# Two transformer layers on one core: work dealt out anew between score slots, rows of maxima sent ahead of the stores, the first layer's norm half a turn earlier, fp4 rounding on GpSimd

## The reference, cut to what matters

```python
xn = layernorm(x)
x = x + attention0(xn) + ffn0(xn)       # ffn0: fp4_linear in and out
xn = layernorm(x)
x = x + attention1(xn) + moe(xn)        # moe: shared expert + top 2 of 8 experts

def fp4_quant_dequant(x):               # blocks of 16 along the last dim
    scale = max(max(abs(xb)) / 6, 1e-12)
    xn = xb / scale                     # rounded to 0, .5, 1, 1.5, 2, 3, 4, 6
    return grid(abs(xn)) * sign(xn) * scale
def fp4_linear(x, w): return fp4_quant_dequant(x) @ fp4_quant_dequant(w).T
ffn0(x) = fp4_linear(silu(fp4_linear(x, w_gate)) * fp4_linear(x, w_up), w_down)
```

## Time and profile before

| | |
|---|---|
| median of 3 runs | 1664.07 us (1662.01 to 1670.28) |
| the profiled execution | 1662.64 us |
| its span, first to last instruction | 1660.9 us |
| busy: PE, DVE, ACT, POOL | 1199.5, 1016.8, 723.0, 375.0 us |
| mean granted TensorE clock | 0.868 of full |
| the chain that ended last | PE 27%, DVE 27%, issue 21%, POOL 9% |

### The profile page before, as it was taken

How to read it: one execution, slowest core, us unless ns; L and a number is a source line. 1 busy time by engine, 2 the same in 40 slices (tenths; PEclk the granted TensorE clock), 3 DMA queues, 4 the chain that set the end, 5 groups by cost and what they waited for, 6 DMA issues and landing times.

```text
span 1660.9 us, 18766 instructions
## 1 busy us (share of the span) xinstructions
PE 1199.5 (72%) x6747; PEld 522.3 (31%) x6807; DVE 1016.8 (61%) x1596; ACT 723.0 (44%) x921; POOL 375.0 (23%) x395
## 2 busy tenths in 40 slices
PE   2657478877786788777867887787778858888851
PEld 1113123212321332223212321232223246677510
DVE  7855677766676767666766676777685425411122
ACT  1045044644464446444644464446454713233450
POOL 5020111101110111011101110111001344455475
PEclk9668668987898889878987798889989979999985
DMA  4934232133313321432133213331410363455332
GB/s 135 349 149 115 89 99 83 30 111 82 85 30 107 95 76 30 112 94 73 29 109 85 84 30 106 80 86 30 113 34 14 96 159 122 131 149 163 110 104 69
DMA packets 143230, 159.65 MB, mean 96 GB/s; under 512 B 14585, under 2 KB 132546, under 8 KB 141090
## 3 DMA queue, kind: packets, MB, share of 16 engines
q1 hardware_dynamic: 129986, 123.87, 26.7%
q0 software_dynamic: 12208, 34.04, 6.9%
q10 hardware_dynamic: 944, 0.54, 0.1%
HBM read 90.11 MB, written 67.76 MB: 95 GB/s over the span
## 4 chain that ended last, share of the span: by engine, by line
PE 27%; DVE 27%; issue 21%; POOL 9%; ACT 6%; DVEq 6%; DMA 3%; SPq 1%; ACTq 0%; POOLq 0%
DVE nm L959 13%; PE sums L347 5%; ACT ex L695 3%; PE mx L359 3%; PE ring L458 3%; PE mx L329 3%; PE mx L409 2%; PE mx L449 2%; PE ring L433 2%; POOL qs L1361 2%; POOL ks L1361 2%; PE ring L253 2%; POOL xn L1313 2%; DVEq L914 1%; DVEq L873 1%
## 5 line engine op out<-in xcount | busy, mean ns | idle before, releaser
L695 ACT ACTIVATE ex<-mx 128x1024 f32<-128x1024 f32 x512 | 512.4, 1025 | 505.4 <-PE mx L359 503.0
L959 DVE TENSOR_REDUCE nm<-mx 128x2 f32<-128x1024 f32 x512 | 600.6, 1216 | 168.8 <-PE mx L329 165.5
L359 PE MATMUL mx<-qs,ks 74*128 74x512 bf16 (+1 forms) x964 | 316.9, 422 | 104.0 <-DMA qs<-nm_hl 52.6
L347 PE MATMUL sums<-ex,vs 128*18 128x512 f32 x2048 | 304.3, 669 | 5.0 <-ACT pv_sb L699 2.6
L329 PE MATMUL mx<-km,qm 32*128 32x512 bf16 x1024 | 151.5, 431 | 83.2 <-DVE nm L959 54.5
L359 PEld LDWEIGHTS mx<-qs,ks 128*128 128x128 bf16 (+1 forms) x1024 | 78.7, 102 | 404.3 <-issue 234.7
L1304 POOL TENSOR_TENSOR rstd<-veps,minus_half 128x4 f32<-128x4 f32 x16 | 16.6, 1038 | 561.3 <-DVE veps L865 561.3
L1340 POOL DMA_INDIRECT xsort<-xn,pos_i x64 | 62.7, 979 | 238.9 <-DVE pos_i L1046 221.8
L1331 POOL TENSOR_TENSOR parts<-qk_f,parts 128x512 bf16<-128x512 f32 x32 | 36.3, 1154 | 321.0 <-DVE parts L876 321.0
L329 PEld LDWEIGHTS mx<-km,qm 32*128 32x128 bf16 x1024 | 36.9, 93 | 222.4 <-DVE nm L959 97.3
L373 PE MATMUL ring<-ident,pv_sb 128*128 128x128 f32 x128 | 21.9, 298 | 59.1 <-DVE att L975 57.6
(11 more groups left out here) (211 smaller groups left out, 1613.8 us busy)
## 6 DMA issues: line engine op xcount, KB each, us to landing
scratch<-parts SPq DMA_DIRECT2D x128, 256.0 KB, 3.6
ks<-scratch SPq DMA_DIRECT2D x64, 256.0 KB
qs<-scratch SPq DMA_DIRECT2D x64, 256.0 KB
xsort<-hs SPq DMA_DIRECT2D x16, 1024.0 KB, 23.5
qm<-scratch SPq DMA_DIRECT2D x64, 128.0 KB, 2.6
km<-scratch SPq DMA_DIRECT2D x64, 128.0 KB, 2.6
rest<-parts SPq DMA_DIRECT2D x32, 128.0 KB, 3.4
ysort<-qs SPq DMA_DIRECT2D x20, 128.0 KB, 1.8
```

What stands on the lines that cost most here:

```text
L347: done = pe.matmul(acc[32 * j:32 * j + 2 * VW, :], values[:, start:start + 2 * VW], ex[:, s % NEX, j, :], start=q == 0 and t == 0, stop=q ...
L359: done = pe.matmul(bank[:, j, :], ks[l][r, h, t * P:(t + 1) * P], qs[l][r, h, :], start=True, stop=True)
L695: act.activation(ex[:, s % NEX, 2 * i:2 * i + 2, :], bank[:, :, :], ACT.Exp, scale=SCALE).then_inc(free, 1)
L959: dve.tensor_reduce(nm[l][:, t, h:h + 2], bank[:, :, :], AX.X, ALU.max, negate=True).then_inc(free, 1)
```

## The change

Four things change. (1) Work moves between slots: in half turn a the FFN's second product and the shared expert's product go from slots 12 to slots 14 and 15, the two halves of the shared hidden product to slots 6 and 7, and of the quantization of h only the second half stays in half turn a; the first half goes to the end of half turn b before it. In half turn b the two gate products stand in two slots. The two transposes of sums, once in one slot, stand in two. The queries and keys are split in two steps. (2) SP sends `load_rows(0, b + 1, 0)` ahead of the stores of layer 1, and the maxima's transposes of both layers come at slot 8. (3) `norm_stats(0, b + 2)` stands in half turn b(b) at slot 7, `normalize(0, b + 2)` at the end of POOL's loop pass b, and `norm0(b + 1)` in a(b) at slot 0 instead of 1. (4) The last three operations of each quantization (add, subtract, multiply by the scale) run on POOL in `round_and_scale`, and one of the two copies of the maxima's rows on ACT.

```diff
@@ PE, work_a (DVE and ACT alike)
-                    if at == (10, "a"):
+                    if at == (11, "a"):
                         ffn_hidden(b, 0)
...
-                    if at == (12, "a"):
+                    if at == (14, "a"):
                         ffn_down(b)
                 if b + 1 <= LAST:
+                    if at == (0, "b"):
+                        norm0(b + 1)
                     if at == (1, "b"):
-                        norm0(b + 1)
-                    if at == (3, "a"):
                         q0(b + 1)
-                    if at == (3, "b"):
+                    if at == (2, "b"):
                         k0(b + 1)
...
-                    if at == (2, "b"):
+                    if at == (3, "a"):
                         sums_transposed(1, b - 2, 2)
...
+                        if at == (3, "b"):
+                            router_hidden(b - 1)
                         if at == (4, "b"):
-                            router_hidden(b - 1)
-                        if at == (5, "b"):
                             router_logits(b - 1)
...
                     if at == (6, "b"):
                         shared_hidden(b - 1, 0)
+                    if at == (7, "b"):
                         shared_hidden(b - 1, 1)
-                    if at == (9, "a"):
+                    if at == (8, "a"):
                         max_rows(1, b - 1, 0)
-                    if at == (12, "b"):
+                    if at == (15, "a"):
                         shared_out(b - 1)
@@ ACT
+            def max_rows(l, b, half):
+                layer, batches = rows_before(l, b)
+                wait(act, rows_in[layer][half], batches * N_ROWS)
+                bank = from_ring(("m", l, b, half))
+                act.copy(nm_hl[:, half, 0, :], bank[0:NH // 2, :]).then_inc(high_ready, 1)
@@ DVE, work_a
-                    for i in range(2):
-                        for step in range(3):
-                            if at == (1 + 3 * i + step + i, "c"):
-                                quantize_h(b, i, step)
+                    if at == (1, "c"):
+                        quantize_h(b, 1, 0)
+                    if at == (7, "c"):
+                        quantize_h(b, 1, 1)
...
-                    if at == (0, "c"):
-                        norm_stats(0, b + 1)
-                    if at == (4, "c"):
-                        split_qk(0, b + 1)
-                    if at == (10, "c"):
+                    if at == (3, "c"):
+                        split_first(0, b + 1)
+                    if at == (5, "c"):
+                        split_second(0, b + 1)
+                    if at == (11, "c"):
                         quantize_x(b + 1, 0)
-                    if at == (11, "c"):
+                    if at == (12, "c"):
                         quantize_x(b + 1, 1)
-                    if at == (13, "c"):
-                        quantize_x(b + 1, 2)
@@ DVE, work_b
-                if at == (10, "c"):
-                    split_qk(1, b)
+                if at == (11, "c"):
+                    split_first(1, b)
+                if at == (12, "c"):
+                    split_second(1, b)
+                if b + 2 <= LAST and at == (7, "c"):
+                    norm_stats(0, b + 2)
...
+                    if at == (13, "c"):
+                        quantize_h(b + 1, 0, 0)
+                    if at == (14, "c"):
+                        quantize_h(b + 1, 0, 1)
@@ POOL
+            def round_and_scale(d, n, qsc, done, count):
+                for op in (ALU.add, ALU.subtract):
+                    pool.tensor_tensor(d, d, binade[:, 0:n], op).then_inc(rounded, 1)
+                    pool.wait_ge(rounded, 2 * count + (1 if op == ALU.add else 2))
+                d3 = d.rearrange("p (k q) -> p k q", q=QB)
+                pool.tensor_tensor(d3, d3, per_block(qsc, n), ALU.mult).then_inc(done, 1)
...
             for b in range(B):
+                if b == 0:
+                    normalize(0, 1)
+                    residual0(1)
                 if b + 1 <= LAST:
-                    normalize(0, b + 1)
-                    residual0(b + 1)
                     third_part(0, b + 1)
+                round_h(b, 1)
                 if b >= 1:
                     scatter(b - 1)
+                if b + 1 <= LAST:
+                    round_x(b + 1)
                 normalize(1, b)
                 residual1(b)
                 third_part(1, b)
+                if b + 1 <= LAST:
+                    round_h(b + 1, 0)
+                if b + 2 <= LAST:
+                    normalize(0, b + 2)
+                    residual0(b + 2)
@@ SP
+                if b + 1 <= LAST:
+                    load_rows(0, b + 1, 0)
                 store_early(1, b)
                 load_max(1, b)
                 store_late(1, b)
-                if b + 1 <= LAST:
-                    load_rows(0, b + 1, 0)
                 load_stacks(1, b, 0)
```

More of the change, by code:

```diff
@@ L185, in two_layers @@
         mx = [ctx.enter_context(nc.psum_tensor(f"mx{i}", [P, 2, 512], FP32)) for i in range(NMX)]
-        ring, pairs = Banks(1), Banks(NMX)
+        ring, pairs, row_sets = Banks(1), Banks(NMX), Banks(1)
         ring_full, ring_free = sem("ring_full"), sem("ring_free")
@@ L335, in max_rows @@
                     pair_read(pe, ("M", l, b, u, i))
+                row_sets.take((l, b, half))
                 transpose_tiles(("m", l, b, half), lambda t: nm[l][:, t, half * 8:half * 8 + 8], cols=NH // 2)
@@ L754, in work_a @@
                         shared_hidden(b - 1, 0)
+                    if at == (7, "b"):
                         shared_hidden(b - 1, 1)
+                    if at == (8, "a"):
+                        max_rows(1, b - 1, 0)
             def work_b(b, k, place):
                 at = (k, place)
+                if b >= 1 and at == (0, "a"):
+                    max_rows(1, b - 1, 1)
                 if at == (1, "a"):
@@ L826, in _ @@
             gates(0, 1)
+            max_rows(0, 0, 0)
             act.wait_ge(weights_in, 16 * N_WEIGHT_DMAS)
@@ L832, in _ @@
             for i in range(SLOTS, NTILE):
+                if i == SLOTS:
+                    max_rows(1, LAST, 1)
                 tile_hidden(i)
@@ L924, in quantize_x @@
                     wait(dve, ring_full, ring.at(("xqT", b - 1))[1] + 1 if b else 0)
+                    wait(dve, xq_ready, b)
+                    wait(dve, h_ready, 2 * b)
                     dve.drain()
-                    quantize_scales(src, T)
+                    quantize_scales(src, T, qsc[0])
                 if step == 1:
-                    quantize_binades(dst, src, T)
-                if step == 2:
-                    quantize_round(dst, T).then_inc(xq_ready, 1)
+                    wait(dve, h_ready, 2 * b)
+                    quantize_binades(dst, src, T).then_inc(xq_scaled, 1)
             def quantize_h(b, i, step):
@@ L934, in quantize_h @@
                 if step == 0:
+                    wait(dve, xq_ready, b + 1)
+                    wait(dve, h_ready, 2 * b + i - 1)
                     dve.drain()
-                    quantize_scales(h, 2 * F0)
+                    quantize_scales(h, 2 * F0, qsc[i])
                 if step == 1:
-                    quantize_binades(h, h, 2 * F0)
-                if step == 2:
-                    quantize_round(h, 2 * F0).then_inc(h_ready, 1)
+                    wait(dve, h_ready, 2 * b + i)
+                    quantize_binades(h, h, 2 * F0).then_inc(h_scaled, 1)
             def ffn_up(b, i):
@@ L961, in max_rows @@
             def max_rows(l, b, half):
-                layer, batches = rows_before(l, b)
-                wait(dve, rows_in[layer][half], batches * N_ROWS)
                 bank = from_ring(("m", l, b, half))
-                dve.tensor_copy(nm_hl[:, half, 0, :], bank[0:NH // 2, :])
-                dve.drain()
+                dve.wait_ge(high_ready, row_sets.at((l, b, half))[1] + 1)
                 dve.tensor_tensor(nm_hl[:, half, 1, :], bank[0:NH // 2, :], nm_hl[:, half, 0, :], ALU.subtract).then_inc(ring_free, 1)
@@ L1272, in _ @@
             quantize_weights(2)
-            for step in range(3):
+            for step in range(2):
                 quantize_x(0, step)
@@ L1282, in _ @@
                 maxima(0, 0, u)
+                if u == 12:
+                    quantize_h(0, 0, 0)
+                if u == 13:
+                    quantize_h(0, 0, 1)
+                if u == 14:
+                    norm_stats(0, 1)
             dve.wait_ge(weights_in, 16 * N_WEIGHT_DMAS)
```

131 lines of the change are left out of this document (76 added, 55 removed).

## The result

The changed kernel takes 1622.51 us (median of 4 runs, 1621.52 to 1626.65) against 1663.04 (1658.34 to 1670.28) of the kernel before, run beside it: ratio 0.9757, 95% interval 0.9717 to 0.9797. The profiled execution took 1621.52 us, 41.1 under the one before (1662.64); the prediction had reckoned 63. So the direction held and the time lies in the wide range of 1560 to 1645 us; it is 2.5 us above the 1580 to 1620 that the forecast gave itself. Two thirds of the forecast gain came.

What follows compares the result with a forecast made beforehand. Half turn a was bound by waits between engines. A period falls from 166.4 to 157.9 us: six give -51, a(0) -6, a(7) -8, the last half turn b +2, together -63, hence 1600 us; range 1560 to 1645.

Steps and rivals of the forecast that it cites:

- the rows' stall and the norm: Start of half turn a: the 5.3 to 5.75 us DMA stall goes; PE waits some 6 us for x, before 4.00.
- The chain T to xn: From T, DVE's second h quantization step ending in b's slot 14: POOL's three operations 5.5 us, then norm 4.3.
- slots 3 to 15: Half turn a: 73.4 us becomes 65.0, walked 61.1 plus 3.9 for low clock; gain 8.4, port wait 1.0 extra.
- changes nothing: Slots 12 to 15 of half turn a: moving the two largest products apart gains nothing, 21.5 us against 21.8.
- Here splitting gains nothing: Slots 6 and 7 of half turn a: 11.2 us as before, with 2.6 for a second pair of table loads.
- I charge one such wait, 1.0 us.: Slots 8 and 9 of half turn a: POOL's rounding of h's second half delays DVE once, 1.0 us.
- a(7), -8: Last half turn a: no next x is normalized, so only the gain of slots 3 to 15, 8 us.
- the last half turn and the tail, +2: Last half turn b: the router, and the scatter the tail waits for, come a slot later, costing 2 us.
- B: Rival: ring, buffer and DVE ties eat 4.2 of 8.4 us, port locks cost two waits: 1637 us, chance 0.20.
- D: Rival: POOL's three roundings before the norm take over 4.5 us each; slower, 1682 us, chance 0.08.
- C: Rival: POOL needs about 4.2 us an operation, norm 7.4 later in six starts: 1655 us, chance 0.07.
- A: Rival: clock stays high in half turn a and POOL's locks cost nothing: 1566 us, chance 0.20.

Runs made afterwards that it cites:

- e10: Changed kernel with h's transposes, down product, gates' transposes and shared output product back in their old slots (10 to 12): 1632.74 us, ratio 0.9815.
- e2: Changed kernel with both shared hidden halves back in slot 6 and both gate pairs back in slot 7: 1589.80 us, ratio 0.9556.
- e1: Changed kernel with the next x's norm and residual ahead of the rounding of h's first half on GpSimd: 1605.52 us, ratio 0.9652.
- e5: Changed kernel with the edits of e1 and e2 together: 1575.99 us, ratio 0.9445.
- the short rounding: Changed kernel with GpSimd rounding only the first 16 columns of h's second half, part of the computation left out: 1593.89 us, ratio 0.9573.
- 1536 us: e5 with binades of h's first half moved to slot 15 of b and scales of its second half to slot 4 of a: 1536.30 us, 0.9225.
- e11: e5 with only the binades of h's first half moved from slot 14 to slot 15 of half turn b: 1540.86 us, ratio 0.9241.

## Why the prediction was right or wrong

**Right: the rows' stall and the norm.** The stall is gone and its gain stayed: the one edit of SyncE's order gives 39 us. The chain T to xn was reckoned as 9.8 us and is 9.1 (T at 508.8, xn at 517.97), TensorE's wait "some 6" and is 5.83. Slots 0 to 2 were to take 25.6 and take 26.4, between 25.6 and 28.1 from half turn to half turn; in a(3), the longest, the key product ran at low clock (2.08 us) behind a wait of 3.00 for the division. (Before the change the statistics of this norm stood at slot 0 of every half turn a that has a next batch, not only of the first.)

**Right sum by luck, wrong terms: slots 3 to 15.** Reckoned 65.0 + 1.0, found 67.4 (the table's four stages). Slots 3 to 5 came nearly as walked (13.3, found 12.5). Slots 12 to 15 were walked at 21.5, which is what they take with the products in their old places (e10); "changes nothing" missed 1.0 there. Two terms failed by more:

- "Slots 6 and 7 ... Here splitting gains nothing" gave 11.2, found 14.3. The walk has 8.6 us of TensorE's work and 2.6 for one pair of loads; with one pair the same slots do take 11.2, so it paid for the first pair only, and the split loses 3.2. In half turn b I split the gates without charging anything: 66.3 reckoned, 67.4 found, and 64.0 with one pair. There the missing price of the split (3.4) hid that the other terms were 2.3 too dear. The two make 6.6 in a period. The profiled execution of e2 shows 4.5, since its slots 0 to 2 and 8 to 11 came out 2.3 longer; with the norm in front (e1 to e5) the same edit gives 5.9.
- "I charge one such wait, 1.0 us." The walk's 15.1 for slots 8 to 11 is about right without the port wait (14.1 with the short rounding), but the changed kernel takes 20.0. That 1.0 + 3.9 comes near the 5.9 is luck: the 3.9 is a lump for all of slots 3 to 15, taken over from the old kernel, whose clock in slots 8 to 11 was low as well (0.70 in a(3)), without any GpSimd operation beside the router's rows. What failed is the price of a wait here: 1.0 was charged for its length, and the low clock behind it costs more.

**Wrong: a(7), -8.** It went from 81.5 to 80.3 us. I gave it the gain of a(3), but before it already ran slots 3 to 15 in 67.9 us and not in 73.4; there was little to win, and the split took 2.2 of that (78.1 with one pair). **Too small: the last half turn and the tail, +2.** From the first exponential of b(7) to the first of the tail it is 292.3 instead of 287.6, where +2 was forecast. The kernel with SyncE's order alone has 286.2, and every kernel with the other parts of the change 290.9 or more (291.1 in e10, with the products back), so it belongs to those parts; which of them was not tried.

**The rivals.** B was nearest, at 1637, and for its second reason: the port costs more than one wait. But its first, that ties of ring and buffers eat the gain, has no support; it was the split of ScalarE's work. Of D the order is real, the roundings in front of the norm, and costs 17 us; but they take 1.4 to 1.7 us each and not over 4.5, so neither D nor C came. A, a clock that stays high, came true only in the experiments: the mean over the run is 0.885 in the changed kernel and 0.914 at 1536 us.

So the missing 22 us are in the account: some 12 in six periods (39.2 won from b(0) to the start of a(7), where 51 were forecast and b(6) was left out of the sum), 6.8 in a(7) and 2.7 in the last half turn, the tail and a(0) with small parts of both signs. What stays open is why slots 0 to 2 and 8 to 11 of one kernel differ from half turn to half turn by 2 to 4 us as the clock falls or stays: in e11 TensorE waits 3.3 us at the same place of a(3) and of a(4), and slots 8 to 11 take 20.8 us at a clock of 0.67 in the one and 17.2 at 0.90 in the other.

## What to carry to other kernels

In a kernel bound by waits, price an added wait twice: by its length and by what TensorE does at low clock after it; the second price varies, as e11 shows. A piece of work that moves to an idle engine must also be looked at in that engine's queue, since what stands behind it may be what another engine waits for; here the norm behind the roundings cost 17 us. And count the table loads whenever ScalarE's work is split over slots, the first pair too.

## What the runs showed of the hardware that was not expected

GpSimd's operation of 128x704 takes 1.38 us with an operand that is broadcast over blocks of 16 and 1.67 with two full ones; VectorE takes 0.89 for each. The first is a multiplication and the others add and subtract, so which of the two makes the difference is not shown. A VectorE subtraction of four columns can take ten times its usual 0.16 us beside GpSimd. And two moves that cost no work, one on VectorE and one on GpSimd, with the table loads brought together, made the kernel 5% faster than the changed one (1540.86 against 1622.51).
